# Sixteen heads on one core: the maxima go in two halves, and the turned scores follow 17 heads behind

## The reference

```
x = x + attn0(layernorm(x)); x = x + moe0(layernorm(x))
# second layer, H = 16 heads of D = 8:
q, k, v = split(layernorm(x) @ W_in.T + b_in)
bias    = minimum((pos[:, None] - pos[None, :]) * slope[h], 8)
scores  = q @ k.T / sqrt(8) + bias
x = x + (softmax(scores) @ v) @ W_out.T + b_out
x = x + moe1(layernorm(x))
```

## Time and profile before

| | us |
|---|---|
| median of 3 timed runs | 1072.15 |
| the profiled execution | 1061.39 |
| its span, first to last instruction | 1059.6 |
| TensorE busy | 806.4 (76%) |
| VectorE busy | 568.2 (54%) |
| ScalarE busy | 383.6 (36%) |
| GpSimd busy | 348.9 (33%) |
| first straight score of the stage | 481.6 |
| first turned score | 512.8 |
| last straight score | 808.2 |
| last turned score | 831.5 |

### The profile page before, as it was taken

One profiled execution on the slowest core, in us unless ns is written; L12 is line 12 of the kernel. 1 busy time (PEld: TensorE's weight loads), 2 busy tenths in 40 slices (PEclk: granted clock), 3 DMA queues, 4 the chain that ended last, 5 costly groups with the idle time before them and its releaser, 6 DMA issues.

```text
span 1059.6 us, 19263 instructions
## 1 busy us (share of the span) xinstructions
PE 806.4 (76%) x5686; PEld 582.4 (55%) x5686; DVE 568.2 (54%) x2230; ACT 383.6 (36%) x886; POOL 348.9 (33%) x560
## 2 busy tenths in 40 slices
PE   0888569999999999525788988998999570018894
PEld 0776445566567777412555656665665370018884
DVE  4677562322322333336678887888885262016673
ACT  0566112222222232000455565556666300015552
POOL 4000517777710333331122113111200205754553
PEclk9999569999999999855789999899999855559998
DMA  9950001112001233145534454345330500011110
GB/s 245 173 167 0 1 3 41 43 38 63 0 0 38 86 108 92 37 98 115 98 74 95 86 100 77 87 97 99 67 62 3 180 1 20 33 49 47 52 51 13
DMA packets 75416, 72.55 MB, mean 68 GB/s; under 512 B 8173, under 2 KB 65984, under 8 KB 73036
## 3 DMA queue, kind: packets, MB, share of 16 engines
q1 hardware_dynamic: 69708, 60.51, 26.2%
q0 software_dynamic: 5632, 11.12, 3.2%
HBM read 43.78 MB, written 27.46 MB: 67 GB/s over the span
## 4 chain that ended last, share of the span: by engine, by line
PE 47%; DVE 15%; issue 12%; DMA 11%; POOL 6%; SPq 3%; ACT 2%; DVEq 2%; POOLq 0%; ACTq 0%
PE bank L1446 9%; PE bank L1447 8%; PE bank L1468 5%; DMA arena<-back_rows 5%; DVE rt L1037 5%; PE bank L1497 3%; PE bank L1585 2%; PE bank L1539 2%; DMA sorted_rows<-arena,send_slot 2%; PE bank L1567 2%; PE bank L1572 2%; DMA qk_parts<-arena 2%; SPq L520 1%; SPq L541 1%; PE bank L1391 1%
## 5 line engine op out<-in xcount | busy, mean ns | idle before, releaser
L1037 DVE CUSTOM_DVE_ANT_0 rt<-bank,alibi 128x256 f32<-128x256 f32 x512 | 192.8, 419 | 39.3 <-PE bank L1539 31.8
L1282 ACT ACTIVATE arena<-bank 128x512 f32<-128x512 f32 x256 | 150.5, 598 | 84.0 <-PE bank L1572 74.1
L945 DVE TENSOR_TENSOR arena<-arena,bank 128x512 f32<-128x512 f32 (+1 forms) x128 | 75.0, 586 | 189.2 <-ACT arena L1255 189.2
L1539 PE MATMUL bank<-arena 72*128 72x256 bf16 x512 | 106.1, 292 | 46.3 <-DVE arena L1037 31.7
L1255 ACT ACTIVATE arena<-bank 128x512 f32<-128x512 f32 (+1 forms) x128 | 66.1, 517 | 203.4 <-PE bank L1447 203.4
L1567 PE MATMUL bank<-arena 81*128 81x256 bf16 x512 | 119.2, 279 | 4.5 <-ACT arena L1282 2.9
L1446 PE MATMUL bank<-arena 128*128 128x320 f32 (+2 forms) x256 | 116.2, 536 | 7.1 <-DVE arena L945 7.1
L1447 PE MATMUL bank<-arena 128*128 128x320 f32 (+2 forms) x256 | 112.0, 519 | 0.0
L1539 PEld LDWEIGHTS bank<-arena 72*128 72x128 bf16 x512 | 36.8, 100 | 99.4 <-DVE arena L1037 70.1
L1572 PE MATMUL bank<-arena,ident_b 128*128 128x256 bf16 (+8 forms) x544 | 84.8, 253 | 0.0
L717 POOL CAST arena<-arena 128x512 bf16<-128x512 f32 x16 | 9.9, 620 | 217.8 <-ACT arena L1303 217.8
(11 more groups left out here) (233 smaller groups left out, 1455.5 us busy)
## 6 DMA issues: line engine op xcount, KB each, us to landing
arena<-qk_parts SPq DMA_DIRECT2D x48, 192.0 KB
arena<-qk_parts SPq DMA_DIRECT2D x144, 64.0 KB
qk_parts<-arena SPq DMA_DIRECT2D x16, 384.0 KB, 2.8
back_rows<-empty_row SPq DMA_DIRECT2D x1, 4096.0 KB, 37.8
arena<-back_rows SPq DMA_DIRECT2D x16, 256.0 KB, 9.4
arena<-in_w SPq DMA_DIRECT2D x2, 2048.0 KB, 11.0
sorted_rows<-empty_row SPq DMA_DIRECT2D x1, 2640.0 KB, 20.4
arena<-sorted_rows SPq DMA_DIRECT2D x40, 66.0 KB, 1.8
```

Source lines behind the costliest of these rows:

```text
L945: nc.vector.tensor_tensor(out, sil[:, k, 0:out.shape[1]], bank[4 + k][:, 0:out.shape[1]], ALU.mult).then_inc(hid_done, 1)
L1037: last = nc.vector.tensor_tensor_reduce(biased[n % 2 * QT + u], bank[n % 2][:, SEQ * u:SEQ * u + SEQ], alibi[:, h, P * (1 - u):P * (1 - u) ...
L1282: nc.scalar.activation(prT3[:, n % (2 * HG)].rearrange("p k t -> p (k t)"), bank[2 + n % 2][:], ACT.Exp).then_inc(exp3_done, 1)
L1539: last = nc.tensor.matmul(bank[n % 2][:, SEQ * u:SEQ * u + SEQ], qs[0:KROWS, c % RING, h, P * u:P * u + P], ks[0:KROWS, c % RING, h, :], s ...
```

## The change

The turned scores follow the straight ones by 17 heads (EXP_LAG), where it was 25. The maxima are handled for eight heads at a time: the four steps from the split to the send take a half batch m (c = m // 2) at offsets 9, 10, 12 and 13 from its first head. In SyncE's loop two sends stand where one stood. Buffers and semaphore counts are halved or doubled to suit. The offsets of `combine`, the statistics and the variance change; what lies behind a batch comes 8 slots earlier through BACK.

```diff
-EXP_LAG = 25
-COMBINE_0, COMBINE_1, STATS, VARIANCE, NORM, TURN, HT, QKV, QK_COPY, VALUES = -41, -40, -39, -38, -33, -30, -29, -26, -25, -19
-SPLIT_MAX_0, SPLIT_MAX_1, TURN_MAX, COPY_MAX = NH + 1, NH + 2, NH + 4, NH + 5
+EXP_LAG = 17
+MH = NH // 2
+COMBINE_0, COMBINE_1, STATS, VARIANCE, NORM, TURN, HT, QKV, QK_COPY, VALUES = -43, -41, -36, -34, -32, -30, -29, -26, -25, -19
+SPLIT_MAX_0, SPLIT_MAX_1, TURN_MAX, COPY_MAX = MH + 1, MH + 2, MH + 4, MH + 5
...
+def half_batch_at(slot, offset):
+
+    m, r = divmod(slot - offset, MH)
+    return m if r == 0 and 0 <= m < 2 * BATCH else None
...
-        def send_max(c):
-
-            wait_apart(sp, (max_rows_done, c + 1))
-            sp.dma_start(qs[MROW:KALL, c % RING], max_rows[0:PARTS * NH, c % 2]).then_inc(max_in[c % 2], 16)
+        def send_max(m):
+
+            c, h = m // 2, MH * (m % 2)
+            wait_apart(sp, (max_rows_done, m + 1))
+            sp.dma_start(qs[MROW:KALL, c % RING, h:h + MH], max_rows[0:PARTS * MH, m % 2]).then_inc(max_in[m % 2], 16)
...
-            send_max(c)
+            send_max(2 * c)
+            send_max(2 * c + 1)
...
-            if h == 0 and c >= 2:
-                dve.wait_ge(max_parts_done, c - 1)
+            if h % MH == 0 and c >= 2:
+                dve.wait_ge(max_parts_done, n // MH - 3)
...
-        def max_parts_0(c):
-
-
-            wait_apart(dve, (max3_done, NH * (c + 1)), *([(max_tr, c)] if c >= 1 else []))
-            nm = nmax3[:, c % 2]
+        def max_parts_0(m):
+
+
+            wait_apart(dve, (max3_done, MH * (m + 1)), *([(max_tr, m)] if m >= 1 else []))
+            nm = nmax3[:, m // 2 % 2, :, MH * (m % 2):MH * (m % 2) + MH]
...
-            if h == 0:
-                pe.wait_ge(max_in[c % 2], 16 * (c // 2 + 1))
+            if h % MH == 0:
+                m = n // MH
+                pe.wait_ge(max_in[m % 2], 16 * (m // 2 + 1))
```

More of the change, by code:

```diff
@@ L264, in _build @@
     nmax3 = carve([P, 2, QT, NH])
-    max_rest = carve([P, QT, NH])
-    max_part = carve([P, QT, PARTS, NH], BF16)
+    max_rest = carve([P, QT, MH])
+    max_part = carve([P, QT, PARTS, MH], BF16)
     max_rows = carve([P, 2, SEQ], BF16)
@@ L1040, in row_max, with max_parts_1 @@
             last.then_inc(max3_done, 1)
-        def max_parts_0(c):
-            wait_apart(dve, (max3_done, NH * (c + 1)), *([(max_tr, c)] if c >= 1 else []))
-            nm = nmax3[:, c % 2]
+        def max_parts_0(m):
+            wait_apart(dve, (max3_done, MH * (m + 1)), *([(max_tr, m)] if m >= 1 else []))
+            nm = nmax3[:, m // 2 % 2, :, MH * (m % 2):MH * (m % 2) + MH]
             nc.vector.tensor_copy(max_part[:, :, 0, :], nm).then_inc(max_split, 1)
-            dve.wait_ge(max_split, 3 * c + 1)
+            dve.wait_ge(max_split, 3 * m + 1)
             nc.vector.tensor_tensor(max_rest, nm, max_part[:, :, 0, :], ALU.subtract).then_inc(max_split, 1)
-        def max_parts_1(c):
-            dve.wait_ge(max_split, 3 * c + 2)
+        def max_parts_1(m):
+            dve.wait_ge(max_split, 3 * m + 2)
             nc.vector.tensor_copy(max_part[:, :, 1, :], max_rest).then_inc(max_split, 1)
-            dve.wait_ge(max_split, 3 * c + 3)
+            dve.wait_ge(max_split, 3 * m + 3)
             nc.vector.tensor_tensor(max_part[:, :, 2, :], max_rest, max_part[:, :, 1, :], ALU.subtract).then_inc(max_parts_done, 1)
@@ L1087, in _ @@
                 row_max(n)
[L1088 to L1091, removed]
+            if (m := half_batch_at(slot3, SPLIT_MAX_0)) is not None:
+                max_parts_0(m)
+            if (m := half_batch_at(slot3, SPLIT_MAX_1)) is not None:
+                max_parts_1(m)
             if (c := batch_at(slot3, COMBINE_0)) is not None:
@@ L1303, in copy_qk, with copy_max @@
             nc.scalar.activation(qkf[:, 1], bank[7][:, SEQ:2 * SEQ], ACT.Identity, bias=bqk[:, 1:2]).then_inc(qk3_done, 1)
[L1305 to L1309, removed]
+        def copy_max(m):
+            act.wait_ge(max_tr, m + 1)
+            if m >= 2:
+                act.wait_ge(max_in[m % 2], 16 * (m // 2))
+            nc.scalar.activation(max_rows[0:PARTS * MH, m % 2], bank[7][0:PARTS * MH, 0:P].bitcast(BF16), ACT.Copy).then_inc(max_rows_done, 1)
         def copy_oT(e):
@@ L1327, in _ @@
                 copy_qk(c)
-            if (c := batch_at(slot3, COPY_MAX)) is not None:
-                copy_max(c)
+            if (m := half_batch_at(slot3, COPY_MAX)) is not None:
+                copy_max(m)
             if (c := batch_at(slot3, COPY_OUT)) is not None:
@@ L1521, in project @@
             if c >= 3:
-                pe.wait_ge(max_rows_done, c - 2)
+                pe.wait_ge(max_rows_done, 2 * c - 4)
             for a in range(2):
@@ L1541, in score, with turn_max @@
             last.then_inc(s3_mm, 1)
[L1543 to L1547, removed]
+        def turn_max(m):
+            pe.wait_ge(max_parts_done, m + 1)
+            if m >= 1:
+                pe.wait_ge(max_rows_done, m)
+            pe.wait_ge(qk3_done, min(m // 2 + 3, BATCH))
             for u in range(QT):
-                last = nc.tensor.transpose(bank[7][0:PARTS * NH, P // 2 * u:P // 2 * u + P // 2].bitcast(BF16),
+                last = nc.tensor.transpose(bank[7][0:PARTS * MH, P // 2 * u:P // 2 * u + P // 2].bitcast(BF16),
                                            max_part[:, u].rearrange("p a h -> p (a h)"), ident_b[:])
@@ L1624, in _ @@
                 project(c)
-            if (c := batch_at(slot3, TURN_MAX)) is not None:
-                turn_max(c)
+            if (m := half_batch_at(slot3, TURN_MAX)) is not None:
+                turn_max(m)
             if (c := batch_at(slot3, TURN_0)) is not None:
```

## The result

The changed kernel takes 1220.5 us (median of 4 runs) against 1070.7 us for the kernel before: a ratio of 1.141 (95% interval 1.136 to 1.146), slower. The forecast was 1233 us, between 1165 and 1275. One of the four runs took 1540.8 us at a granted clock of 0.55 and is left out of the ratio; the other three lie between 1218.9 and 1222.1.

A forecast was written before the change was run, and what follows sets the result against it. Bound: a loop through SyncE's queue, no engine full; project to release 24.0 us plus 9.0 back, 13 periods of 33.0. The stage ends 161 us later: 1061.39 + 161 = 1222, plus 10.8 for the median: 1233 us, between 1165 and 1275.

The forecast's parts named there:

- SyncE comes to the send 14.1 us after `project`: SyncE's queue: project and copy 1.9, split 4.7, store 2.9, twelve copies 4.2, given rows' issue 0.4 us precede the send.
- The release is 24.0 us after `project`: TensorE's wait at the first turned score: 23.2 us to the given rows' landing plus 0.8, against 14.6 available.
- A send behind the copies is late by them: SyncE's queue: the send of the first eight maxima lands behind the twelve copies, 9.4 us more than the 14.6 there.
- The row of batch 12: Profile's nearest case, a send behind copies without given rows: 5.80 us for 24 KB, TensorE starting 14.05 us after first copy's issue.
- From the release to `project` 9.0 us: TensorE's stretch of turned and straight scores, `turn`, `weigh`, `turn_max` at low clock: 9.0 us; 6.4 at full clock.
- The period is 33.0 us, 13 of them: Attention stage's loop from `project` to `project`: 24.0 + 9.0 us, bounds 30.4 and 36.2, 13 periods between 14 late releases.
- The sum: Whole kernel: profiled execution 1061.39 us + 161 = 1222; 10.8 more on the median's scale gives 1233 us.
- What costs nothing: Doubled maxima instructions on VectorE, TensorE, ScalarE, SyncE: hidden by the hole, otherwise at most 12 us; shorter lag gains 7 us.
- A: Rival: TensorE's clock does not fall, or is back at once; period 30.4 us, total 1197 us; chance 0.13.
- B: Rival: the send lands unhindered, 2.8 us after its issue; middle period 24.6 us, total 1115 us; chance 0.12.
- C: Rival: the send is in time, landing within 14.6 us of `project`; total 1065 to 1077 us; chance 0.05.

The follow-up runs named there:

- e9_third: The changed kernel, but from batch 4 on replicate issues only four of the twelve copies, sends still behind copies and given rows: 1129.9 us, 1.044.
- e3_early: The changed kernel, but SyncE sends the first half of the maxima between the landed store and the twelve copies: 1125.8 us, 1.050.
- e5_pool_send: The changed kernel, but GpSimd issues the sends of the maxima, each as soon as copied; SyncE keeps stores, copies and given rows: ratio 1.035.
- e11: Repeat of e7_early_given (lag 17) on the same chip as e10, against the kernel before: 1056.1 us, 0.977.
- e10: e7_early_given with EXP_LAG 25 instead of 17, nothing else: 1047.0 us, 0.969 of the kernel before.
- e7_early_given: The changed kernel with the first half sent before the twelve copies and load_given(c + 4) ahead of replicate(c + 2): 1049.2 us, 0.980 of the kernel before.

## Why the prediction was right

The mechanism was the one forecast, and the time came within 13 us. By its terms:

- *SyncE comes to the send 14.1 us after `project`.* 633.42 less 619.35: 14.1; over 13 periods 13.5 to 15.9, mean 14.4.
- *The release is 24.0 us after `project`.* 23.3 in the period shown; over 13 periods 22.0 to 24.9, mean 23.8. The way to it was in part luck: I took the landing of the given rows and 0.8 us to get past them. The send does not wait for them: it landed ahead of them in the period shown, and the last two rounds, which have no given rows ahead, waited 10.0 and 8.4 us for it like the rest (8.1 to 10.6). Both wait beside the same copies, and that is why the one could stand for the other.
- *A send behind the copies is late by them.* Shown three ways: e9_third (fewer copies, earlier), e3_early (in front of them, no hole), e5_pool_send (another queue, mostly). The row of batch 12 was the right one to lean on: its release came 14.05 us after the first copy's issue, and those of the changed kernel 12.6 to 15.3, mean 14.2. The Trainium skill's ring order (DMA: Bandwidth & Descriptors, Queues, rings and completion order) agrees with that: in all 14 rounds TensorE waited 8.6 us or more for the send. The same section says that an engine takes turns between the queues it has work for, a packet at a time; e5_pool_send agrees, with sends that landed 3.2 to 9.4 us after their issue beside the traffic. How much of the lateness is the order within the queue and how much the sharing of the DMA engines, no run separates.
- *From the release to `project` 9.0 us.* 6.9 in the first period, where nothing is turned back or weighed yet, then 8.5 to 9.6; mean of the 13 periods 9.0. The low clock lasted 3.5 to 6.0 us after the release, 4.8 in the mean, and not about 6. What that saves is in part made up by a term that the sum had left out: four transposes of an earlier batch (`turn_back`, L1606) take 0.5 us of this stretch. TensorE waits for no engine in it.
- *The period is 33.0 us, 13 of them.* 32.7. The last release came at 938.36 (941 forecast), the last turned score at 990.1 (992).
- *The sum.* 1222 us against the profiled execution's 1218.9. The 10.8 us that were added for the scale of the median mostly did not come: the median is 1220.5, 1.6 above that execution. That is 9 of the 12 us by which 1233 is off; the other 3 are the period. The execution of the kernel before that I worked from was among its quickest, and the changed kernel's runs that the ratio uses hardly spread (1218.9 to 1222.1).
- *What costs nothing.* In the changed kernel, right. But the price of the parts that the hole hid was off: I had 7 us of gain for 8 slots less of lag. With hardly a stall left, the shorter lag cost 9 us instead (1056.1 against 1047.0, e11 and e10): I had taken the slot's length as not depending on the lag. Why it does stays open.
- *Rivals.* A (clock stays up): the stretches show 0.50. B (the send lands unhindered): no, and on a queue of its own only at times. C (in time): no.

## What to carry to other kernels

Before a consumer is moved earlier, follow its input back to the queue that issues it, and count what stands ahead of that issue in the program: here one send moved ahead of the copies took back 95 of the 150 us (e3_early), the given rows moved ahead as well took back the rest (e7_early_given), and that swap alone gave 22 us to the kernel before. A wait that an in-order queue makes for one transfer is a wait for all that stand behind it, so the transfer whose input is ready first belongs first (the given rows), and a small urgent one needs a gap in the traffic as well as a place ahead of it. If a load is behind a wait in the chain and the issuing queue had been idle shortly before, it can be issued in that gap.

## What the runs showed of the hardware

- A 12 KB transfer between two places of the on-chip memory, issued from a queue of its own, takes 1.8 us when nothing runs beside it, and up to 9.4 us beside 1152 KB of copies and 256 KB of given rows (e5_pool_send). Behind the copies on SyncE's queue it takes 8.1 to 10.6 us.
- Moving 256 KB from behind to ahead of the twelve copies hardly moved the send behind both (1211 us against 1220), and a third of the copies moved it much (1130 us). Whether it is the bytes of the copies or the many small rows they move, no run separates.
- Landings need not follow the order of issue on SyncE's queue: given rows issued at 632.91 landed at 643.2, the send issued behind them at 633.42 landed at 642.6.
- The granted clock fell from 1.00 to 0.50 within 13 of the 14 holes, 1.8 to 3.2 us after TensorE's last product and before any work came back (in the first it was low already), and rose 3.5 to 6.0 us after the release.
